# Contracting an attention table by halves between the units that build it, with the third quarter's remainders made for 16 batches first

## The reference

```python
h = take(weight.T, x)                                  # (64, 128, 64): one row of a 256-row table for each token
h = h + attention(layernorm(h))                        # sigmoid attention over 8 heads, then relu(. @ Wo)
h = h + mixture(layernorm(h))                          # router, best two of six experts, three layers each
```

## Time and profile before

| | |
|---|---|
| median of 3 runs | 247.37 us |
| the runs | 247.05, 247.37, 250.84 us |
| the profiled execution, its own time | 249.88 us |
| its span, first to last instruction | 248.1 us |
| mean granted TensorE clock in it | 0.959 |
| TensorE busy | 211.6 us, 85% of the span |
| VectorE busy | 159.6 us, 64% |
| ScalarE busy | 106.6 us, 43% |
| GpSimd busy | 77.8 us, 31% |

### The profile page before, as it was taken

One profiled execution on the slowest core, in us unless ns is written; L12 is line 12 of the kernel. 1 busy time (PEld: TensorE's weight loads), 2 busy tenths in 40 slices (PEclk: granted clock), 3 DMA queues, 4 the chain that ended last, 5 costly groups with the idle time before them and its releaser, 6 DMA issues.

```text
span 248.1 us, 5974 instructions
## 1 busy us (share of the span) xinstructions
PE 211.6 (85%) x2394; PEld 88.3 (36%) x2398; DVE 159.6 (64%) x331; ACT 106.6 (43%) x188; POOL 77.8 (31%) x122
## 2 busy tenths in 40 slices
PE   0477876699899989998986889999999999998892
PEld 0354533034433433334542424434342523232210
DVE  3424673236795794798379498879889785928161
ACT  1228631123353353351245346555655555454530
POOL 4000465243352263303554307170625323201010
PEclk9999999569979988999999999999999999999997
DMA  7632399999698689710010669677663919384751
GB/s 144 147 121 53 81 223 239 262 264 260 178 260 209 174 225 262 194 68 18 3 42 4 168 154 213 137 161 162 164 156 103 210 53 242 77 215 104 180 132 42
DMA packets 26282, 37.85 MB, mean 153 GB/s; under 512 B 15888, under 2 KB 17104, under 8 KB 26256
## 3 DMA queue, kind: packets, MB, share of 16 engines
q1 hardware_dynamic: 19376, 19.92, 33.6%
q0 software_dynamic: 5216, 16.98, 26.4%
q10 hardware_dynamic: 1664, 0.58, 1.2%
HBM read 17.79 MB, written 2.83 MB: 83 GB/s over the span
## 4 chain that ended last, share of the span: by engine, by line
PE 60%; DVE 13%; DMA 9%; issue 9%; ACT 5%; POOL 2%; POOLq 1%; SPq 0%; DVEq 0%; ACTq 0%
PE PS L662 11%; PE PS L686 10%; PE PS L826 8%; PE PS L815 7%; PE PS L800 7%; DMA G<-Gs 5%; PE PS L746 3%; DVE Htab L954 2%; PE PS L698 2%; PE PS L837 2%; DMA WB<-gate_scratch 2%; ACT OT L566 2%; DMA cst<-consts 2%; PE PS L610 1%; PE PS L757 1%
## 5 line engine op out<-in xcount | busy, mean ns | idle before, releaser
L229 POOL DMA_DIRECT2D G<-Gs x64 | 33.6, 530 | 63.1 <-ACT Gs L472 56.8
L662 PE MATMUL PS<-A,BD 32*32 32x256 f32 x1024 | 35.8, 410 | 9.7 <-ACT Gs L472 6.4
L1071 DVE SCALAR_TENSOR_TENSOR H2g<-PS,nb_s,WB 128x1024 f32<-128x1024 f32 x24 | 30.8, 1283 | 13.6 <-PE PS L815 10.9
L488 ACT ACTIVATE H<-PS,b_s 128x512 f32<-128x512 f32 x48 | 30.2, 679 | 11.8 <-PE PS L800 11.8
L998 DVE COPY Gs<-PS 128x512 f32<-128x512 f32 x32 | 20.9, 686 | 21.0 <-PE PS L662 12.0
L686 PE MATMUL PS<-G,cnt 128*64 128x512 f32 x128 | 33.6, 662 | 0.0
L472 ACT ACTIVATE Gs<-PS 128x512 f32<-128x512 f32 x32 | 17.6, 595 | 33.3 <-PE PS L662 29.4
L400 POOL TENSOR_TENSOR GP<-GG,GP 32x512 fp32r<-32x512 f32 x8 | 10.2, 1269 | 66.2 <-ACT GP L504 66.2
L800 PE MATMUL PS<-X,W1s 64*128 64x512 f32 x96 | 27.1, 641 | 1.3 <-ACT H L488 1.3
L815 PE MATMUL PS<-H,W2s 64*64 64x512 f32 x192 | 26.1, 614 | 1.5 <-DVE H2g L1071 1.5
L826 PE MATMUL PS<-H2g,W3s 128*64 128x512 f32 x96 | 25.7, 616 | 0.9 <-DVE Y L1132 0.5
(11 more groups left out here) (114 smaller groups left out, 289.1 us busy)
## 6 DMA issues: line engine op xcount, KB each, us to landing
G<-Gs POOLq DMA_DIRECT2D x64, 256.0 KB, 6.5
WB<-gate_scratch SPq DMA_DIRECT2D x48, 256.0 KB, 5.3
xb<-ids_scratch SPq DMA_DIRECT2D x8, 256.0 KB, 3.8
h_out<-Y SPq DMA_DIRECT2D x8, 256.0 KB, 2.7
GG<-gate_scratch SPq DMA_DIRECT2D x64, 12.0 KB
vo_scratch<-VOs SPq DMA_DIRECT2D x2, 256.0 KB, 2.1
VOr<-vo_scratch SPq DMA_DIRECT2D x4, 128.0 KB, 3.1
wk_s<-wk SPq DMA_DIRECT2D x2, 128.0 KB, 5.0
```

Source lines behind the costliest of these rows:

```text
L229: eng.dma_start(G2[half % G2_RING][first::8, :, :], Gs[n % GS_RING][:, m, :]).then_inc(sent[n % GS_RING][m], 16)
L488: ins = act.activation(H1[q][:, u * HT:(u + 1) * HT], PS[:, B_L1 + u, :], ACT.Relu, bias=b1_s[:, u, q:q + 1])
L662: ins = pe.matmul(PS[32 * x:32 * x + 32, B_G + i, w * NV:(w + 1) * NV], BD[n % BD_RING][rows, x].rearrange("p c f -> p (c f)")[:, w::2], A ...
L1071: dve.scalar_tensor_tensor(out=H2g[q][:], in0=two_banks(l2_bank(q)), scalar=nb2_s[:, q:q + 1], in1=WB[s % RING][:, q, :], op0=ALU.max, op1 ...
```

## The change

`place(n)` takes the place of `contraction_after(n)`. The contractions begin after unit 5 (`BEHIND` = 5) and are spread over all units: in the four units from unit 5, 9 and 13 on, those of one quarter are done by halves. Positions 0 to 3 hold: (0) the lower halves of m and m + 1; (1) their upper halves and the lower half of m + 2; (2) the turn of m, the lower half of m + 3, the upper half of m + 2, the turn of m + 1; (3) the upper half of m + 3, the turn of m + 2; the turn of m + 3 opens the next position 0. The work of ScalarE and VectorE is placed to match. The lower half of a `G2` quarter is written again after `lower_done`, which the lower half of the quarter's fourth contraction increments. The third quarter's parts are made in two pieces (`PARTS`): for the first 16 batches (`FIRST`) where they stood, for the other 48 after VectorE's `cut`, together with the rest of the last `table_rows`, which itself is made for 8 batches first. GpSimd makes its first `cut` before it clears `GG`. The gather of step 2 waits for the second piece. The first `keep_warm` has 7 matmuls where it had 10.

```diff
+PARTS = ((0, 0, NB), (1, 0, NB), (2, 0, FIRST), (2, FIRST, NB))
@@ send_unit
             if half >= G2_RING and n % 2 == 0:
-                eng.wait_ge(o_ps, 4 * ((half - G2_RING) // 2 + 1))
+                if half % 2 == 0:
+                    eng.wait_ge(lower_done, (half - G2_RING) // 2 + 1)
+                else:
+                    eng.wait_ge(o_ps, 4 * ((half - G2_RING) // 2 + 1))
...
+        def place(n):
+            return (4 * ((n - BEHIND) // 4), (n - BEHIND) % 4) if n >= BEHIND else (0, -1)
@@ gpsimd
             pool.wait_ge(o_ps, NF * 4)
-            pool.wait_ge(h_tab, NF * 4 * VK)
-            for i in range(RING):
-                pool.memset(GG[i][:], 0.0).then_inc(gg_zero, 1)
+            pool.wait_ge(h_tab, NF * 4 * VK + VK)
...
+            cut(1)
+            pool.wait_ge(cut_pool, 3)
+            for i in range(RING):
+                pool.memset(GG[i][:], 0.0).then_inc(gg_zero, 1)
             pool.wait_ge(gg_zero, RING)
-            cut(1)
             normalise(0)
@@ scalar, in the loop over the units, behind the copies of banks 0 and 1
-                if n % UPF in (1, 2) and n > 2 * UPF:
-                    middle(n // UPF - 2, n % UPF - 1)
-                for m in contraction_after(n):
+                m, at = place(n)
+                if at == 1:
                     o_evac(m)
+                    o_evac(m + 1)
+                    if m >= 4:
+                        for k in range(VK):
+                            middle(m // 4 - 1, k)
+                if at == 2:
+                    o_evac(m + 2)
+                if at == 3:
+                    o_evac(m + 3)
+            o_evac(4 * (NF - 1) - 1)
             for k in range(VK):
-                middle(NF - 2, k)
+                middle(2, k)
...
+            middle(3, 0)
             take_h(0)
+            middle(3, 1)
             squares(0)
@@ tensor
                     if k == 1:
                         ins.then_inc(o_ps, 1)
+                    elif j == 3:
+                        ins.then_inc(lower_done, 1)
...
-                if n % UPF == 0 and n >= 2 * UPF:
-                    turn(n - UPF - 1)
-                for m in contraction_after(n):
-                    contract(m, range(VK))
-                    if m % 4:
+                m, at = place(n)
+                if at == 0:
+                    if m >= 4:
                         turn(m - 1)
-            turn(4 * (NF - 1) - 1)
-            for m in range(4 * (NF - 1), 4 * NF):
+                    contract(m, (0,))
+                    contract(m + 1, (0,))
+                if at == 1:
+                    contract(m, (1,))
+                    contract(m + 1, (1,))
+                    contract(m + 2, (0,))
+                if at == 2:
+                    turn(m)
+                    contract(m + 3, (0,))
+                    contract(m + 2, (1,))
+                    turn(m + 1)
+                if at == 3:
+                    contract(m + 3, (1,))
+                    turn(m + 2)
+            m = 4 * (NF - 1)
+            contract(m - 1, (1,))
+            turn(m - 2)
+            contract(m, (0,))
+            turn(m - 1)
+            for m in range(4 * (NF - 1) + 1, 4 * NF):
                 contract(m, (0,))
             for m in range(4 * (NF - 1), 4 * NF):
                 contract(m, (1,))
@@ gather
+                if i * TB == FIRST:
+                    pe.wait_ge(lo_ok, VK * len(PARTS))
...
-            keep_warm(10)
+            keep_warm(7)
@@ vector, in the loop over the units
-                if n % UPF == 0 and n >= 2 * UPF:
-                    table_rows(n - UPF - 1)
-                if n >= 2 * UPF:
-                    if n % UPF < 2:
-                        remainder(n // UPF - 2, n % UPF)
-                    else:
-                        low(n // UPF - 2, n % UPF - 2)
-                for m in contraction_after(n):
-                    if m % 4:
+                m, at = place(n)
+                if at == 0:
+                    if m >= 8:
+                        low(m // 4 - 2, 1)
+                    if m >= 4:
                         table_rows(m - 1)
+                if at == 1 and m >= 4:
+                    for k in range(VK):
+                        remainder(m // 4 - 1, k)
+                if at == 2:
+                    table_rows(m)
+                    table_rows(m + 1)
+                if at == 3:
+                    if m >= 4:
+                        low(m // 4 - 1, 0)
+                    table_rows(m + 2)
@@ vector, behind the units
+            for k in range(VK):
+                low(1, k)
+            table_rows(4 * (NF - 1) - 2)
             table_rows(4 * (NF - 1) - 1)
             for k in range(VK):
-                remainder(NF - 2, k)
+                remainder(2, k)
             one_hot_ids(0)
             one_hot_ids(1)
             for k in range(VK):
-                low(NF - 2, k)
-            for m in range(4 * (NF - 1), 4 * NF):
+                low(2, k)
+            for m in range(4 * (NF - 1), 4 * NF - 1):
                 table_rows(m)
+            table_rows(4 * NF - 1, 0, TB)
...
             cut()
             dve.wait_ge(sel_dve, 2)
+            table_rows(4 * NF - 1, TB, NB)
+            for k in range(VK):
+                remainder(3, k)
             centre(0)
             variance(0)
+            for k in range(VK):
+                low(3, k)
             normalise(0)
```

More of the change, by code:

```diff
@@ L49 @@
 BH = NB // 2
+BEHIND = 5
+FIRST = 16
+PARTS = ((0, 0, NB), (1, 0, NB), (2, 0, FIRST), (2, FIRST, NB))
 HEAD_ORDER = (0, 2, 4, 6, 1, 3, 5, 7)
@@ L202, in build @@
         gg_ld = [sem(f"gg_ld{i}") for i in range(RING)]
+        lower_done = sem("lower_done")
         gg_zero, gp_hi, gp_ready = sem("gg_zero"), sem("gp_hi"), sem("gp_ready")
@@ L252, in l2_bank, with part_of_table @@
             return B_X if q == 2 else B_L2
-        def contraction_after(n):
-            fg, r = divmod(n, UPF)
-            if fg == 0 or r < 2:
-                return ()
-            m = 4 * (fg - 1) + 2 * (r - 2)
-            return (m, m + 1)
+        def place(n):
+            return (4 * ((n - BEHIND) // 4), (n - BEHIND) % 4) if n >= BEHIND else (0, -1)
+        def part_of_table(ap, p, k):
+            q, b0, b1 = PARTS[p]
+            return ap[:, k, b0:b1, q * FB:(q + 1) * FB]
         def o_bank(m):
@@ L460, in o_evac, with middle @@
                 act.activation(O1[m % 2][:], PS[:, o_bank(m), :], ACT.Relu).then_inc(o_sb, 1)
-            def middle(q, k):
-                act.wait_ge(rem_ok, VK * q + k + 1)
-                act.activation(Hmid[:, k, :, q * FB:(q + 1) * FB], rem[:, k], ACT.Copy).then_inc(mid_ok, 1)
+            def middle(p, k):
+                b0, b1 = PARTS[p][1:]
+                act.wait_ge(rem_ok, VK * p + k + 1)
+                act.activation(part_of_table(Hmid[:], p, k), rem[:, k, b0:b1], ACT.Copy).then_inc(mid_ok, 1)
             for n in range(UNITS):
@@ L944, in counts_out, with table_rows @@
                                     PS[32 * u:32 * u + NC, 5, :].rearrange("a (b n) -> a n b", n=NC)).then_inc(cnt_sb, 1)
-            def table_rows(m):
+            def table_rows(m, b0=0, b1=NB):
                 fg, j = divmod(m, 4)
@@ L953, in table_rows @@
                     src = PS[:, B_OT + m % 2, :].rearrange("p (f k u b) -> p k u f b", k=VK, u=2, b=NB)[:, k]
-                    dve.tensor_tensor(o, src, e.unsqueeze(3).broadcast_to([P, 2, 2, NB]), ALU.add).then_inc(h_tab, 1)
+                    dve.tensor_tensor(o[:, :, :, b0:b1], src[:, :, :, b0:b1],
+                                      e.unsqueeze(3).broadcast_to([P, 2, 2, b1 - b0]), ALU.add).then_inc(h_tab, 1)
             def mixture_weights(n):
@@ L974, in mixture_weights, with remainder @@
                                                  op0=ALU.mult, op1=ALU.add).then_inc(bias_dve, 1)
-            def remainder(q, k):
-                f = slice(q * FB, (q + 1) * FB)
+            def remainder(p, k):
+                q, b0, b1 = PARTS[p]
                 dve.wait_ge(h_tab, VK * 4 * (q + 1))
@@ L981, in remainder, with low @@
                     dve.wait_ge(lo_ok, VK * (q - 1) + k + 1)
-                dve.tensor_tensor(rem[:, k], Htab[:, k, :, f], upper(Htab[:])[:, k, :, f], ALU.subtract)\
-                   .then_inc(rem_ok, 1)
-            def low(q, k):
-                f = slice(q * FB, (q + 1) * FB)
-                dve.wait_ge(mid_ok, VK * q + k + 1)
-                dve.tensor_tensor(Hlo[:, k, :, f], rem[:, k], Hmid[:, k, :, f], ALU.subtract).then_inc(lo_ok, 1)
+                dve.tensor_tensor(rem[:, k, b0:b1], part_of_table(Htab[:], p, k), part_of_table(upper(Htab[:]), p, k),
+                                  ALU.subtract).then_inc(rem_ok, 1)
+            def low(p, k):
+                b0, b1 = PARTS[p][1:]
+                dve.wait_ge(mid_ok, VK * p + k + 1)
+                dve.tensor_tensor(part_of_table(Hlo[:], p, k), rem[:, k, b0:b1], part_of_table(Hmid[:], p, k),
```

(1 more changed line is left out.)

## The result

The changed kernel took 245.09 us in the median of 4 runs (242.96 to 247.32), the kernel before 247.49 us: a ratio of 0.987 (0.983 to 0.992), 1.3% faster. Forecast were 240.9 us and 238.8 to 244.9. So it is a little faster, by 2 to 3 us (5 in one later group) and not by 6.5, and the measured time lies just above the range. A median here is that of all executions, while a ratio and its interval leave out those more than 1.5% above the fastest of the same kernel, so the two can differ by half a per cent.

What follows compares the result with a forecast made beforehand. DMA and TensorE took turns in the table stage, neither full. With DMA full, `cut` ends at 106.9; + 131.2 + 1.0 = 239.1 us of span, + 1.8 outside = 240.9 us; range 238.8 to 244.9.

Steps and rivals of the forecast that it cites:

- At 262 to 265 GB/s that is 49.6 to 49.0 us: Table stage from 48 us: the remaining sends at full DMA rate, last byte at 97.0 to 97.6 us.
- c: End of the last piece of VectorE's `cut`, where the batches' steps begin; 116.9 us before, forecast 106.9.
- rival A: TensorE's clock falls again around the last landing, up to 1.7 us, with slipped slots 2: 242.9 us; chance 0.26.
- the 98.7 of the forecast: Time in us of the last send's landing in the table stage, including 0.3 for an earlier `x_load`.
- my 12.99 MB: Data still to be sent in the table stage at 48 us, from 58.5 us x 222 GB/s.
- `low(3, .)` lies beside GpSimd's power: 0.: After `cut`: VectorE's 1.85 us of low parts is covered by GpSimd's 2.1 us power work, costing 0.
- The change leaves those nearly alone.: The 131.2 us from the end of `cut` to the end of the span stay nearly the same.
- I carry no correction over.: The profiled execution lay 2.5 us above the median 247.4; the forecast 240.9 was not corrected for it.
- rival C: Table stage: no DMA limit, landings come early, TensorE alone bounds, turn 15 ends at 103.5: 239.5 us; chance 0.05.
- D: TensorE's clock pauses spread through the table stage; with 24 us of low clock 251 us; chance 0.04.
- 7 us of queue to spare: Table stage: of up to 12 us of queued sends, 7 us remain to ride out an uneven slot.
- B: VectorE sets the table stage's pace, late copies losing two microseconds in each of the last two quarters: 245; chance 0.10.

Runs made afterwards that it cites:

- e2: The changed kernel again, without an edit; 245.68 us, ratio 0.994 to the kernel before.
- e5: The changed kernel, but GpSimd sends unit 12 only when all of unit 11 has landed, a pause of the DMA queue; 246.93 us.
- e7: The changed kernel with `low(3, .)` moved behind step 0's `normalise` and GpSimd's four clears behind its second `cut`; 243.85 us.
- e9: The changed kernel a third time, without an edit; 243.06 us, ratio 0.974 to the kernel before.
- e13: The changed kernel with a pause of the DMA queue ahead of unit 8's sends; 245.34 us, one run.
- e15: The changed kernel without a pause, run beside two versions with one; 246.60 us, one run.
- e4: The kernel before with the third quarter's pieces, later clears and 7 warm matmuls added, keeping its own order of units; 247.83 us, ratio 0.9955.
- e8: The changed kernel with ten more unused warm matmuls in step 0; 241.71 us, ratio 0.977 to the kernel before.
- e1: The kernel before again, without an edit, for a second profile; 246.87 us.
- e6: The changed kernel with at most 8 sends in flight from unit 5 on, where 12 were; 245.06 us, ratio 0.984 to the kernel before.
- e12: The changed kernel's order of halves without the pieces, later clears and 7 warm matmuls, plus ten warm matmuls in step 0; 241.79 us, ratio 0.975.
- e14: The changed kernel with the pause ahead of unit 12's sends again; 250.67 us, one run.

## Why the prediction was wrong

**The DMA rate, the term that was mis-sized most.** "At 262 to 265 GB/s that is 49.6 to 49.0 us." The step was right in kind: DMA is full from the start to the last send, and c is the last landing + 8.3 us where the clock holds (forecast 8.2): 8.3 in the first profile, e2, e5, e7, e9 and e13. But the rate at full share is not a constant. The earlier trace rows showed it only in stretches of 3 to 16 us; I took that of the two longest for 49. Uninterrupted it was 246, 252, 253 and 257 GB/s (64 to 92 us) in the changed kernel's four profiles. c was 109.4, 110.2, 108.3 and 109.7, on average 109.4, 2.5 us over the 106.9 (0.4 of it is e15's 1.7 us of rival A, over four profiles). The last landings were at 101.0, 101.9, 100.0 and 99.7, on average 2.0 later than the 98.7 of the forecast. By my estimate the rate is enough for that: from 48 to 97 us it was 247, 248, 256 and 255, and my 12.99 MB take 51.7 us at their mean and 49.3 at 263.5. Three of the four rates lie below even my low bound of 255 GB/s.

**Behind c.** "`low(3, .)` lies beside GpSimd's power: 0." It does lie beside it, and stops it: 0.57 us on the first instruction and 0.54 on the second. With 0.57 at the copy of H (forecast 1.0: VectorE and ScalarE were a little quicker than I worked out) and the clears just ahead, 1.75 us instead of 1.0. It is the most regular number of the study: 9.2 us from c to `normalise` in every kernel with the pieces where they stand, 7.4 to 7.5 in every one without them, 8.0 in e7.

**The steps.** "The change leaves those nearly alone." From `normalise` to the end were 123.7 and 123.9 us before, and 125.8, 123.7, 125.2 and 125.9 in the changed kernel, on average 1.4 us more. The three long ones have 6.8 us of low clock around 134 us, e2 has 3.4. The fall lies between the second `normalise` and the fourth. That stretch took 28.1 to 28.3 us with 6.8 us of low clock (e4 too), 26.8 to 26.9 with 3.4 (28.6 in e8, which stays unexplained) and 26.6 to 27.1 with none (e7, whose edit changes this stretch, is left out); so the fall is about 1.0 of the 1.4 us. The other 0.4 lie behind the last `normalise`, which takes 33.2 to 34.3 us in every kernel, whatever the clock did before. I had looked for the clock only in the table stage. Why it falls there in every profile with the new order or the pieces and without the ten extra warm matmuls, and in neither of the two of the kernel before, stays open; TensorE's two waits just ahead of it (1.0 and 1.1 us) are as long in both.

The three together: 240.9 + 2.5 + 0.75 + 1.4 = 245.5 us. The terms are means of the four profiled executions, which took 245.6 on average, so the sum closes on those; that it also meets the median of 245.3 says that they are ordinary ones.

**The comparison with the median.** "I carry no correction over." For the forecast of the new time that was right; the gain against the median rested on it too, and e1 shows that an ordinary execution of the kernel before already has c at 114.2. So the forecast gain of 6.5 us would have been 6.3 from e1's own steps (114.2 - 106.9 - 1.0), and 4.65 us of it went into the three terms above. That leaves some 1.6 us, where the medians of the result are 2.4 us apart; the remaining 0.8 are within what two executions of one kernel differ by.

**Smaller slips.** In rival C turn 15 ends at 103.5, but TensorE's own limit was worked out as 104.5, so C would have been 240.5 and not 239.5. In D 24 us of low clock cost 12, which makes 252.9 and not 251. And `x_load` was issued at 101.3, 101.0, 98.4 and 98.4 us in the changed kernel's four profiles, in the first behind the last landing and in the others 0.9 to 1.7 us ahead of it; whether it cost anything is not shown.

**What held.** The added waits in `send_unit` cost nothing, TensorE's quarter fell from 20.2 to 16.5 us, the clock held from 58 to 97 us in all four profiles, VectorE left the end of the chain, and e6 shows that not even 12 sends in flight were needed (I had counted 7 us of queue to spare; 4 us less made no difference). Rival A came true in one of the changed kernel's four profiles and cost its 1.7 us. B and D did not come. C was excluded by every window: no rate near 435 GB/s, 320 GB/s at most (e1, 48 to 52 us).

## What to carry to other kernels

When two resources take turns in a stage, spreading the work of one between the pieces of the other can win about the smaller of the two gaps (here 3.7 of 4.2 us a quarter), but size it by the rate that the busier one holds over the whole stage, with the low end of its spread, and not by its best stretch. Work that is moved beside another engine is hidden only if the two do not share a port: look first for two-input VectorE instructions beside GpSimd ones. And before a gain is set against a median, ask whether the profiled execution is an ordinary one: one more profile of the kernel before would have shown the 2.7 us.

## What the runs showed of the hardware

- At a full DMA share the rate of these transfers from SBUF to SBUF (256 KB each, 16 target partitions) differs between executions of one program and within one: 222 to 320 GB/s over 4 us without a pause (222 in e12, 40 to 44 us; 320 in e1, 48 to 52; 312 from 44 to 56 us in e1 and 263 in the first profile of the same kernel), with a mean over 28 us between 245 (e6) and 275 (e8). Behind a moment of empty engines it was 277 to 284 over 10 to 14 us (e5, e13, e14); the link to the pause is likely, not proved.
- GpSimd instructions that read SBUF stood still beside VectorE's two-input instructions: 0.25 became 0.81, 1.67 became 2.22 and a cast of 0.40 became 1.00 us (before, the changed kernel, e7). VectorE was held up in its turn: two `low` of 1.82 us took 2.44 beside GpSimd's `cut` (e7).
- A fall of TensorE's clock to 1.2 GHz for 6.8 us made the two steps around it 28.1 to 28.3 us long in four profiles (the first, e4, e9, e15), where five without a fall had 26.6 to 27.1; one of 3.4 us left them at 26.8 to 26.9 in seven profiles and went with 28.6 in an eighth (e8).
